# Macaron layer on eight cores: weight casts spread anew, another head with zero products, and 12 layer norm tiles transposed by transfers from ScalarE's queue

## The reference, cut to what matters

```python
x = L0_attn_batch                                    # per core 2048 x 1024
x = x + 0.5 * ffn(layernorm(x), w_gate, w_up, w_down)   # int32 weights / 127, hidden 3072
x = x + attn(layernorm(x), Wq, Wk, Wv, Wo, omega, W1, b1, W2, b2, gamma, beta)
x = x + 0.5 * ffn(layernorm(x), w_gate, w_up, w_down)

def ffn(x, wg, wu, wd):
    return (silu(x @ wg.T) * (x @ wu.T)) @ wd.T
def attn(x, ...):          # 16 heads of 64, causal linear attention with 128 features
    q, k, v = x @ Wq, x @ Wk, x @ Wv                 # features exp(omega q - max)
    a = causal_linear_attention(q, k, v) @ Wo
    h = gamma * (x + a - mean) / sqrt(var + 1e6) + beta
    return relu(h @ W1 + b1) @ W2 + b2               # 1024 -> 4096 -> 1024
```

## Time and profile before

| | us |
|---|---|
| median of 3 runs (lowest, highest) | 1813.14 (1812.77, 1820.92) |
| the profiled execution's own time | 1805.6 |
| its span, first to last instruction, slowest core (core 4) | 1804.0 |
| span of the fastest core (core 7) | 1782.2 |
| TensorE busy in core 4 | 1752.6 |

### The profile page before, as it was taken

One profiled execution on the slowest core, in us unless ns is written; L12 is line 12 of the kernel. 1 busy time (PEld: TensorE's weight loads), 2 busy tenths in 40 slices (PEclk: granted clock), 3 DMA queues, 4 the chain that ended last, 5 costly groups with the idle time before them and its releaser, 6 DMA issues.

```text
span 1804.0 us, 29674 instructions; the slowest of 8 cores (1782.2 to 1804.0 us)
## 1 busy us (share of the span) xinstructions
PE 1752.6 (97%) x9232; PEld 832.5 (46%) x9232; DVE 774.6 (43%) x1697; ACT 442.9 (25%) x982; POOL 186.6 (10%) x354
## 2 busy tenths in 40 slices
PE   5999999999998899999999999999999999999999
PEld 2444444444554344444444444444444444444444
DVE  5453115511785244666465433567533110431341
ACT  2221002202553125422332430233241130010110
POOL 3111101100021130103000000300001110000000
PEclk9999999999999999999999999999999999999999
DMA  9998957999999965787556775746666564544543
GB/s 201 238 224 170 190 152 153 188 217 204 238 180 170 191 201 153 171 185 189 167 149 177 186 208 179 198 141 175 173 192 192 170 178 153 171 158 154 199 152 105
DMA packets 198901, 324.54 MB, mean 180 GB/s; under 512 B 125792, under 2 KB 125920, under 8 KB 198752
## 3 DMA queue, kind: packets, MB, share of 16 engines
q1 hardware_dynamic: 185936, 277.49, 55.0%
q0 software_dynamic: 12240, 44.11, 17.1%
q10 hardware_dynamic: 576, 1.05, 0.2%
HBM read 311.12 MB, written 52.43 MB: 202 GB/s over the span
## 4 chain that ended last, share of the span: by engine, by line
PE 92%; DMA 5%; SPq 1%; DVE 1%; issue 1%; ACT 1%; DVEq 0%; POOL 0%; ACTq 0%; POOLq 0%
PE d_ps L876 35%; PE d_ps L916 31%; PE d_ps L893 17%; DMA fmZ<-aotm 3%; PE a_ps L989 2%; PE d_ps L989 2%; DMA x_tm<-xin 2%; SPq L322 1%; PE a_ps L450 1%; PE a_ps L548 1%; PE a_ps L451 1%; ACT ftm L471 0%; DMA ring<-gu_i 0%; PE a_ps L574 0%; PE a_ps L502 0%
## 5 line engine op out<-in xcount | busy, mean ns | idle before, releaser
L916 PE MATMUL d_ps<-ring,big 128*128 128x512 bf16 x2176 | 488.1, 380 | 0.1
L916 PEld LDWEIGHTS d_ps<-ring,big 128*128 128x128 bf16 x2176 | 207.5, 98 | 233.6 <-issue 1.9
L876 PE MATMUL d_ps<-fmX,ring 128*128 128x512 bf16 x1152 | 267.6, 383 | 1.2 <-ACT fmX L347 1.2
L1053 ACT ACTIVATE th_t<-d_ps 128x512 f32<-128x512 f32 x192 | 115.0, 599 | 617.8 <-PE d_ps L876 616.2
L876 PE MATMUL d_ps<-fmZ,ring 128*128 128x512 bf16 x1152 | 255.7, 379 | 0.1
L1164 DVE SCALAR_TENSOR_TENSOR th_t<-th_t,d_ps 128x512 f32<-128x512 f32 x192 | 131.6, 685 | 210.0 <-ACT th_t L1053 209.5
L471 ACT ACTIVATE ftm<-a_ps,nmax 128x128 bf16<-128x128 f32 x512 | 146.3, 369 | 242.4 <-DVE nmax L458 238.2
L876 PE MATMUL d_ps<-fmY,ring 128*128 128x512 bf16 x768 | 169.5, 379 | 1.4 <-ACT fmY L347 1.4
L876 PEld LDWEIGHTS d_ps<-fmZ,ring 128*128 128x128 bf16 x1152 | 110.6, 98 | 126.2 <-issue 0.2
L876 PEld LDWEIGHTS d_ps<-fmX,ring 128*128 128x128 bf16 x1152 | 109.9, 99 | 122.4 <-issue 6.2
L893 PE MATMUL d_ps<-fmX,ring 128*128 128x512 bf16 x640 | 143.5, 379 | 0.0
(11 more groups left out here) (80 smaller groups left out, 1376.8 us busy)
## 6 DMA issues: line engine op xcount, KB each, us to landing
ring<-gu_b SPq DMA_DIRECT2D x144, 512.0 KB, 4.1
ring<-w_b SPq DMA_DIRECT2D x128, 512.0 KB, 3.9
ring<-d_b SPq DMA_DIRECT2D x72, 512.0 KB, 4.4
w_b<-w_f POOLq DMA_DIRECT2D x32, 512.0 KB, 12.5
ring<-gu_i POOLq DMA_DIRECT2D x24, 512.0 KB, 11.5
gu_b<-ring SPq DMA_DIRECT2D x24, 512.0 KB, 17.7
ring<-q_b SPq DMA_DIRECT2D x16, 512.0 KB, 10.4
ring<-k_b SPq DMA_DIRECT2D x16, 512.0 KB, 9.3
```

Source lines behind the costliest of these rows:

```text
L876: r = e.matmul(d_ps[bank][:, :], ring[:, so + g * 1024 + k * 128:so + g * 1024 + (k + 1) * 128], xT[:, k * 512:(k + 1) * 512], start=(k == ...
L916: r = e.matmul(d_ps[t][:, :], lhs[:, o:o + 128], ring[:, so + i * 512:so + (i + 1) * 512], start=(s == 0 and i == 0), stop=(s == n_slots - ...
L1053: e.activation(th_t[:, (n % 2) * 512:(n % 2 + 1) * 512], d_ps[2 * (n % 2)][:, :], AF.Tanh, scale=TANH_SC).then_inc(s_tanh, 1)
```

## The change

Head: the x tiles 0 and 1 and then the identity are loaded first; TensorE multiplies zeros (30 products, then 3 between transposes) while it has nothing to do; tile 1 is scaled by ScalarE in place of VectorE; the first pair runs in two halves of 256 columns, the first as soon as two tiles are there; GpSimd issues slots 2 to 7 later, behind the statistics of block 1. LN1 of block 1 is done at ticks 2 to 8 in place of 0 to 10.

Twelve tiles (LN1 of block 2, LN2 of block 0, LN1 of block 3) are no longer transposed on TensorE and copied by ScalarE but by a DMA transpose that ScalarE issues. Casts: 22 places inside attention of block 0 become 11; 6 go into the first down product, 10 in place of 12 into the next gate and up, 5 in place of 3 into q and k, 4 into `wo(0)`, 2 behind it. W2's casts have two semaphores, so that its first half can be loaded without the second.

```diff
-        XBAR0 = 20
+        XBAR0 = 8
...
-        def sp_ln_transpose(e, which, b, j):
+        def dma_ln_transpose(e, which, b, j):
             m = ln_no(which, b) + j
             dst = ln_order[m // 4][2]
             e.wait_ge(s_lxf, m + 1)
-            if j == 0:
-                e.wait_ge(*((s_v, 16), (s_v, 32), (s_w1, 32), (s_up, 120), (s_w1, 64),
-                            (s_up, 144), (s_w1, 96))[m // 4 - XBAR0 // 4])
+            if j == 0 and m > XBAR0:
+                e.wait_ge(*((s_up, 48), (s_up, 48), (s_v, 16), (s_v, 32), (s_w1, 32),
+                            (s_up, 120), (s_w1, 64), (s_up, 144),
+                            (s_w1, 96))[m // 4 - XBAR0 // 4 - 1])
...
+        def act_ln_tick_dma(e, which, b, k, k0, stride, lag=2):
+            for j in ln_at(k, k0 + lag + 1, stride):
+                dma_ln_transpose(e, which, b, j)
...
-                if b == 0 and s % 7 in (1, 4):
+                if b == 0 and s % 7 == 1:
                     cast_piece(e)
...
+            pool_ln_rstd(e, LN1, 1, 1)
+            e.wait_ge(s_x[6], 16)
+            e.dma_start(slot(3), slots[3][0], max_dma_last_dim=8192).then_inc(s_lc[3], 16)
+            pool_ln_rstd(e, LN1, 1, 2)
+            pool_ln_rstd(e, LN1, 1, 3)
+            for n in range(4, RING):
                 e.dma_start(slot(n), slots[n][0], max_dma_last_dim=8192).then_inc(s_lc[n], 16)
...
+            for i in range(6, 12):
+                e.wait_ge(s_d, 8 * i)
+                cast_piece(e)
             for i in range(N_GU):
...
-                if i % 2 == 0:
+                if i % 12 in (1, 3, 5, 8, 10):
                     e.wait_ge(s_up, 48 + i)
                     cast_piece(e)
...
                 if b == 0:
-                    for i in range(3):
+                    for i in range(N_O):
+                        e.wait_ge(s_wo, 4 * i + 1)
                         cast_piece(e)
...
                     pool_rstd(e, sti_no(b) + j, 1e6)
+                if b == 0:
+                    cast_piece(e)
+                    cast_piece(e)
...
+            def busy(n):
+                for i in range(n):
+                    e.matmul(d_ps[3][:, :], zero[:, 0:128], zero[:, :], start=True, stop=True)
+            e.wait_ge(s_zero, 1)
+            busy(30)
+            e.wait_ge(s_id, 16)
             for j in range(4):
                 pe_ln_transpose(e, LN1, 0, j, j)
+                if j < 3:
+                    busy(3)
             def first(k):
-                pe_ln_tick(e, LN1, 1, k, 0, 2)
-                pe_ln_tick(e, LN1, 2, k, 24, 6, 5)
+                pe_ln_tick(e, LN1, 1, k, 2, 1, 1)
...
             def second(k):
-                if k == 0:
-                    e.wait_ge(s_up, 48)
-                act_ln_tick(e, LN2, 0, k, 0, 4)
-                act_ln_tick(e, LN1, 3, k, 18, 4)
+                act_ln_tick_dma(e, LN2, 0, k, 0, 6)
+                act_ln_tick_dma(e, LN1, 3, k, 26, 5)
```

More of the change, by code:

```diff
@@ L102, in build @@
         warm = sbuf("warm", 1, F32)
+        zero = sbuf("zero", 512, BF16)
+        nmr = sbuf("nmr", 1, F32)
         bst = sbuf("bst", 24, F32)
@@ L756, in sp_program @@
                 for which, b, j in ln_turn[n]:
-                    sp_ln_transpose(e, which, b, j)
+                    dma_ln_transpose(e, which, b, j)
                 for b, j in i_turn[n]:
@@ L781, in build @@
                   + [(w1_b, w1_f, i, s_cw1) for i in range(N_W1)]
-                  + [(w2_b, w2_f, i, s_cw2) for i in range(N_W2)])
+                  + [(w2_b, w2_f, i, s_cw2[i // 8]) for i in range(N_W2)])
         n_cast = [0]
@@ L801, in pool_program @@
             pool_ln_rstd(e, LN1, 0, 3)
-            for n in range(2, RING):
+            e.dma_start(slot(2), slots[2][0], max_dma_last_dim=8192).then_inc(s_lc[2], 16)
+            pool_ln_rstd(e, LN1, 1, 0)
+            pool_ln_rstd(e, LN1, 1, 1)
[4 more added lines that the diff above has]
+            for n in range(4, RING):
                 e.dma_start(slot(n), slots[n][0], max_dma_last_dim=8192).then_inc(s_lc[n], 16)
             e.dma_start(omT[:, :], omD_in).then_inc(s_om, 16)
-            for j in range(4):
-                pool_ln_rstd(e, LN1, 1, j)
             for n in range(RING, SL_GU2):
@@ L828, in pool_program @@
                 cast_piece(e)
-            for i in range(3):
-                e.wait_ge(s_qk, 5 * i + 1)
+            for i in range(5):
+                e.wait_ge(s_qk, 3 * i + 1)
                 cast_piece(e)
@@ L881, in pair, with first_pair @@
                     side()
+            def first_pair(so):
+                st["pair"] += 1
+                for half in range(2):
+                    e.wait_ge(s_lev, 2 * half + 2)
+                    for g in range(2):
+                        for k in range(8):
+                            o = k * 512 + half * 256
+                            r = e.matmul(d_ps[g][:, half * 256:(half + 1) * 256],
+                                         ring[:, so + g * 1024 + k * 128:
+                                              so + g * 1024 + (k + 1) * 128],
+                                         fmX[:, o:o + 256], start=(k == 0), stop=(k == 7))
+                        if half:
+                            r.then_inc((s_gate, s_up)[g], 1)
+                for g in range(2):
+                    freed[g] = ((s_gm, 1), (s_h, 1))[g]
             def column_groups(xT, n_slots, done, evicted, n0, side):
@@ L994, in pe_program @@
                 freed[t] = (s_dx, 8 + t + 1)
-            def second(k):
-                if k == 0:
-                    e.wait_ge(s_dx, 16)
-                pe_ln_tick(e, LN2, 0, k, 0, 4)
-                pe_ln_tick(e, LN1, 3, k, 18, 4)
-            side = Ticks(second)
-            gu(LN1, 2, fmZ, side)
-            down(72, 16, side)
+            gu(LN1, 2, fmZ, quiet)
+            down(72, 16, quiet)
             q_part(0, fmY, quiet)
```

80 lines of the change are left out of this document (50 added, 30 removed).

## The result

The changed kernel takes 1865.99 us (median of 5 runs, 1858.87 to 2168.48), the kernel before 1820.92 beside it (5 runs, 1812.77 to 1907.95). The ratio of the undisturbed runs is 1.024, with a 95% interval of 1.021 to 1.027: slower by 2.4%, where 1788 us and a gain were forecast. The profiled execution took 1862.89 us; its span is 1861.0 us in core 7, the slowest, and 1832.6 in core 1, the fastest. (A few executions of either kernel fell in a disturbed state of the chip, hence the high ends; the ratios leave them out.)

What follows compares the result with a forecast made beforehand. TensorE was taken as the bound, idle mainly before the first transposes and in attention of block 0. 1804.0 - 23 - 5.4 - 5.5 + 5 + 7 = 1782, 1784 as device time, plus 4: 1788 us, range 1775 to 1811.

Steps and rivals of the forecast that it cites:

- the term of ScalarE's queue: Twelve tiles transposed by DMA from ScalarE's queue: two or three stops of TensorE, +7 us taken from 0 to 45.
- relief: At the twelve tiles, a stopped TensorE frees its loads, and 1 us of empty DMA passes 40 packets; halves stops in a row.
- rival 1: At the twelve tiles, ScalarE's queue becomes the new stop: 12 to 30 us, chance 0.18; more, chance 0.14.
- Rival 2: At the twelve tiles, the queue serves a tile in bundles, so no stop: 1781 us, chance 0.10.
- The casts' term: Attention of block 0: with 11 casts instead of 22, both waits and both slow starts go, -23 us.
- Where the casts go: At W1 of block 0, two casts behind norm I's statistics delay its transposes: 0 to +10 us, taken +5.
- Rival 3: `wo(0)` and W1 of block 0 wait 10 to 15 us, or some of 23 us stays: 1798 to 1804, chance 0.12.
- The head's term: Start of the kernel: block 1's pass begins near 43.5 to 44 us instead of 49.3, -5.5 us.
- Rival 4: The head does nothing for the slowest core, since slots come late: 1793 us; counted inside the forecast's chance of 0.46.
- The transposes' term: Twelve tiles no longer transposed on TensorE between pairs, 0.45 us each: -5.4 us.

Runs made afterwards that it cites:

- run with four places: Changed kernel with four places instead of two for a normalised tile, for the 12 tiles on ScalarE's queue: 1868.66 us, ratio 1.028.
- casts cut small: Changed kernel with GpSimd's queue DMAs (first pass's loads and all casts) cut at 1,024 elements instead of 8,192, same bytes: 1855.09 us, ratio 1.0209.

## Why the prediction was wrong

**The step that failed** is the term of ScalarE's queue: "So the stop per tile is 0 (gaps in the share) to 30 - 19 - 3.7 = 7 us, halved by the relief for those in a row ... I take +7 us, two or three stops". The mechanism before it was right: one packet a turn, near 60 turns (66 counted), about 30 us for a tile (31.1 the median of the first pass). Its size in stops was wrong: 53.8 us in core 7, 4.5 us a tile. Another 8.1 us stand in the down product behind them, in a wait whose releaser the profile doesn't show; the loads `ring<-d_b` issued from 425 to 449 us took 27.5 us to land (4.1 over the whole span), so a late load is likely and not shown. That is rival 1, whose case of 4 us a tile was given 1829 us, and stops of more than 30 us a chance of 0.14.

Three things in that step did not hold. It reckoned a tile's landing at 30 us, that of a tile on an empty queue, against 19 us of slack in `lntm`. The three landings that VectorE waited for took 31.8, 36.0 and 45.8 us, and three of the five stops, 35.3 us, follow them (7.71, 15.47 and 12.11). One stop of some 7 us was right by the formula; 7 us for all twelve tiles was not. And the formula has no term for the blocked issue, though the prediction had both its signs: 40 packets left for each engine when the next tile comes, and issues of 11 to 18 us on SyncE. On ScalarE such issues took 13.8 and 16.7 us, four times the 3.7 us that a tanh can wait, and the other two stops follow them (7.04 and 11.49, 18.5 us). The run with four places shows that the queue's rate, not `lntm`, is the limit. Third, the "relief" hardly came. From 124 to 130 us, inside the stop that ends at 138.75, the queues still moved 143 packets of GpSimd's, 136 of SyncE's and 143 of ScalarE's: all three had a backlog, and a stopped TensorE didn't take it away. From 350 to 440 us, with TensorE idle for a third of the time, the DMA share is 1.19.

Rival 2, the tile in bundles, is refuted: it wanted a landing near 4 us and several packets of the transpose for each one of the others. The landing took 31.1 us, and the packets were 408 for 405 and 407. The Trainium skill, "DMA: Bandwidth & Descriptors", section "Queues, rings and completion order", says that an engine goes round its queues by whole packets of some nine to seventeen descriptors. For a DMA transpose beside stores this trace disagrees: its 256-byte pieces, each a packet of its own in the records, take one turn each. Bundles of equal number in all queues would give the same counts, but not the same spread. From 117 to 131 us in core 6, 14.6 packets of ScalarE's queue start in each half microsecond, and the variance of that number is 1.08 times its mean, as for single packets; with bundles of nine on 16 engines it would, by estimate, be several times the mean.

The other terms can be read from the start of the first product of each part, here as lengths in us, the mean of the eight cores of one profiled execution each.

| | block 1 starts | from there to first down | down, block 2 to q | q, k, v and attention of block 0 to `wo(0)` | `wo(0)` to W1 |
|---|---|---|---|---|---|
| before | 44.5 | 150.9 | 210.8 | 220.9 | 43.5 |
| changed | 46.9 | 171.2 | 241.5 | 206.9 | 53.3 |
| changed, tiles on TensorE | 46.6 | 156.7 | 210.8 | 203.5 | 54.2 |
| casts alone | 46.3 | 151.6 | 210.7 | 203.3 | 54.6 |
| head alone | 47.4 | 155.6 | 211.4 | 226.3 | 43.5 |
| head, old order of loads | 50.2 | 150.3 | 215.1 | 225.3 | 43.5 |
| 17 casts, none at `wo(0)` | 45.8 | 151.0 | 210.8 | 202.8 | 41.4 |

**The casts' term** (-23) was right: the waits for `aotm` above 2 us and the slow starts are gone with the respread casts (but for 7.7 us in one core with the casts cut small), and the stretch up to `wo(0)` is 17.6 us shorter with the casts alone (21.8 in core 4, for which the term was made). **Where the casts go** (+5) was too small: 11.1 us in the last column. The wait at W1 is 7.3 us in core 7 of the changed kernel but 16.6 in core 6, and 10.8 to 14.8 in the runs with the casts alone and with the tiles back on TensorE. The prediction priced the two casts behind norm I and not the four at Wo, whose packets were still queued when the transposes were issued; the run without all six has no such wait and is 1.2% of the time better (0.9817 against 0.9937, from two sets of runs). Rival 3 thus came true beside rival 1.

**The head's term** (-5.5) was wrong at its first step. Block 1 starts at 47.76 us in core 7 of the changed kernel (45.3 to 48.5 in all cores), where 43.5 to 44 was forecast; the pair at 44.31 is still one of block 0.

```profile
44.31 3.61 PE L913 MATMUL d_ps<-fmX,ring 128*128 128x512 bf16 x16 [1.10 <-DMA ring<-gu_i]
47.76 3.62 PE L913 MATMUL d_ps<-fmY,ring 128*128 128x512 bf16 x16
```

The prediction reckoned from core 4, the latest before with 49.30. In the mean of the cores block 1 starts at 44.5 to 46.3 us with the old head and at 46.6 to 47.4 with the new one, and the pass behind it is 5 us longer, as the loads come late. That is +8 us alone; beside the new casts the ratios differ by less than they can tell (0.9945 against 0.9937), though the same 5 us stand in the table (156.7 against 151.6). Rival 4 was nearer.

**The transposes' term** (-5.4) could not be seen by itself; their pieces are gone from TensorE after 60 us.

The sum with measured terms: 1788, plus 54 - 7 for the stops, 8 for the down product, 2 for W1 in core 7 (7.3 in place of 5), and 5.5 to 13.5 for the head, is 1850.5 to 1858.5. The median is 1866. Of what is left, 8 to 15 us, the slow clock after the stops is the most: at 0.216 us each, the 355 products of the window from 60 to 160 us would take 76.7 us and the 250 from 350 to 440 us 54.0, and TensorE was busy for 80.86 and 60.82, together 11 us more. The mean granted clock of the cores is 0.978 to 0.985, against 0.992 to 0.998 before. The prediction priced the slow clock for no stop of ScalarE's queue.

## What to carry to other kernels

Before a transfer of many small packets gets a queue of its own, count its turns: packets per DMA engine times the summed packet time of all busy queues (38 us by that for 30.7 measured, so it is on the long side). If that is longer than the distance to the next such transfer, the issue will block the engine that issues it, and on an engine that feeds TensorE every blocked microsecond beyond its slack is lost; put such transfers where the casting queue is quiet (2.9 us here), or leave the work on TensorE (0.45 us). When bulk casts are moved, ask of each new place which small, urgent transfer is issued in the next two casts' time. And the first products of a head can start sooner while the next block starts later; read the start of every block in every core, not in the one that was latest.

## What the hardware showed that was not expected

- With three queues busy, a queue of 256-byte packets gets one for each packet of 3.6 KB of the others (408 to 405 and 407), and a tile of 256 KB lands in 31.1 us in the median and up to 45.8; on SyncE's own queue the median was 10.6, up to 32.8. Its packets themselves took 0.03 us each in the first pass and 0.13 in gate and up of block 2 (45.8% of the 16 engines over 135 us, 7497 packets); why is not shown.
- Pieces of 504 bytes written in place of 3.6 KB cost a cast about 0.08 us each and not 0.35: its queue used 79.1% of the engines for 5.55 MB where 43.6% did for 5.12.
- A DMA share of 1.04 or 1.05 over 110 us went with no stop of TensorE in two kernels; the stops for `aotm` lay in a stretch with 1.11.
